# A Mamba block between two ternary feed-forwards: where POOL's u times B stands in each slot

## The reference

```python
x = x + 0.5 * ffn(layernorm(x), W_up, W_gate, W_down)
x = x + mamba(layernorm(x), ...)
x = x + 0.5 * ffn(layernorm(x), W_up, W_gate, W_down)

def ffn(x):            # weights quantised to {-1, 0, 1} * mean(|W|), 2048 hidden units
    hidden = silu(x @ wu.T) * (x @ wg.T)
    return hidden @ wd.T

def mamba(resid):      # E = 1024 channels, N = 16 states per channel
    r = rmsnorm(resid) * norm_w
    skip, x_in = r @ W_skip, r @ W_in
    x = silu(causal_conv4(x_in) + conv_b)
    delta = softplus(x @ W_delta_1 @ W_delta_2 + b_delta_2)
    Bm, Cm = x @ W_B, x @ W_C
    h[l] = h[l-1] * exp(delta[l] * A) + (delta[l] * x[l]) * Bm[l]   # for each e, n
    y[l] = sum_n h[l, e, n] * Cm[l, n]
    return resid + ((y + x * W_D) * silu(skip)) @ W_out
```

## Time and profile before

| | |
|---|---|
| median of 3 runs | 3043.34 us (3043.31 to 3052.29) |
| the profiled execution's own time | 3045.95 us |
| its span, first to last instruction | 3044.2 us |
| busy: PE, DVE, POOL, ACT | 92%, 89%, 65%, 59% |
| chain that ended last: PE, DVE, issue, ACT, POOL | 64%, 20%, 6%, 3%, 1% |
| mean granted TensorE clock | 0.975 |

### The profile page before, as it was taken

The page is one execution under the profiler, slowest core; times in us unless marked ns, Lnnn a source line. Parts: engine busy times, 40 slices in busy tenths (PEclk is TensorE's granted clock), DMA queues, the critical chain, the costliest instruction groups (busy, mean ns, idle before and its releaser), DMA issues.

```text
span 3044.2 us, 53491 instructions
## 1 busy us (share of the span) xinstructions
PE 2796.4 (92%) x18791; PEld 2192.2 (72%) x18791; DVE 2709.3 (89%) x3613; ACT 1809.8 (59%) x4212; POOL 1993.6 (65%) x1875
## 2 busy tenths in 40 slices
PE   4777899999999999999999999999999999999888
PEld 3556677776877777787777768777777877777655
DVE  6359898999999999998999899999999989999992
ACT  6255656565565656556565655656565565656551
POOL 2165676757677675767777576776757677775761
PEclk9888899999999999999999999999999999999888
DMA  6010101001010100101010010101001010100100
GB/s 252 28 32 18 32 22 36 18 22 43 15 39 22 36 18 22 43 17 37 21 36 18 22 43 15 39 22 36 18 22 43 17 38 22 36 18 22 35 29 8
DMA packets 53313, 99.88 MB, mean 33 GB/s; under 512 B 7804, under 2 KB 9144, under 8 KB 52536
## 3 DMA queue, kind: packets, MB, share of 16 engines
q1 hardware_dynamic: 53048, 96.45, 10.1%
HBM read 87.78 MB, written 8.65 MB: 32 GB/s over the span
## 4 chain that ended last, share of the span: by engine, by line
PE 64%; DVE 20%; issue 6%; ACT 3%; POOL 1%; DVEq 0%; ACTq 0%; POOLq 0%
PE ps L1415 17%; PE ps L1426 14%; PE ps L1438 11%; PE ps L1377 10%; DVE h L1164 8%; PE ps L1491 6%; DVE y L1190 4%; DVE xc L1233 2%; PE ps L1447 2%; PE ps L1454 2%; PE ps L1464 2%; DVE act L1206 1%; DVE act L1198 1%; DVE xw L1256 1%; ACT ps L880 1%
## 5 line engine op out<-in xcount | busy, mean ns | idle before, releaser
L647 POOL TENSOR_TENSOR h<-u,bb 128x1024 f32<-128x1024 f32 x512 | 1222.1, 2387 | 305.5 <-PE ps L1377 298.4
L880 ACT ACTIVATE ps<-delta,a_neg 128x255 f32<-128x255 f32 x2048 | 882.4, 466 | 664.1 <-DVE h L1164 662.2
L1164 DVE TENSOR_TENSOR_SCAN h<-ps,h 128x512 f32<-128x512 f32 x1024 | 1191.8, 1205 | 33.3 <-POOL h L651 17.6
L1190 DVE SCALAR_TENSOR_TENSOR y<-ps,ccur,y 128x512 f32<-128x512 f32 x960 | 670.3, 739 | 46.9 <-PE ps L1377 45.9
L1377 PE MATMUL ps<-ident,h 128*128 128x128 f32 x4096 | 564.1, 280 | 97.4 <-DVE y L1190 93.2
L1377 PEld LDWEIGHTS ps<-ident,h 128*128 128x128 f32 x4096 | 475.7, 144 | 183.8 <-issue 80.4
L1415 PE MATMUL ps<-xh,q_gate 128*128 128x256 f16 x2048 | 462.4, 273 | 37.5 <-DVE act L1198 22.6
L1415 PE MATMUL ps<-xh,q_up 128*128 128x256 f16 x2048 | 466.6, 275 | 15.9 <-DVE xl L1103 12.9
L1415 PE MATMUL ps<-xl,q_up 128*128 128x256 f16 x2048 | 466.7, 275 | 0.0
L1415 PE MATMUL ps<-xl,q_gate 128*128 128x256 f16 x2048 | 462.1, 273 | 0.0
L742 POOL TENSOR_TENSOR hl<-act,hh 128x512 f16<-128x512 f32 x256 | 300.9, 1178 | 233.5 <-ACT hh L905 233.5
(11 more groups left out here) (133 smaller groups left out, 3449.4 us busy)
## 6 DMA issues: line engine op xcount, KB each, us to landing
bb<-b_scratch SPq DMA_DIRECT2D x224, 256.0 KB, 3.2
xs<-in_L_attn_resid_dram SPq DMA_DIRECT2D x17, 512.0 KB, 3.8
out_dram<-xs SPq DMA_DIRECT2D x16, 512.0 KB, 4.3
wraw<-in_L_ffn_W_up_dram SPq DMA_DIRECT2D x4, 1024.0 KB, 8.9
wraw<-in_L_ffn_W_gate_dram SPq DMA_DIRECT2D x4, 1024.0 KB, 13.1
wraw<-in_L_ffn_W_down_dram SPq DMA_DIRECT2D x4, 1024.0 KB, 14.2
w_in<-in_L_attn_W_in_dram SPq DMA_DIRECT2D x1, 2048.0 KB, 21.6
w_skip<-in_L_attn_W_skip_dram SPq DMA_DIRECT2D x1, 2048.0 KB, 8.8
```

The lines of the kernel that those rows point to most:

```text
L647: pl.tensor_tensor(h[:, s % RING, :, :], u[:, :, :], bb[:, planes_of(s) % 2, s % PLANES:s % PLANES + 1, :].broadcast_to([P, HE, CH]), ALU. ...
L880: ins = ac.activation(abar[r][:, e, 1:], delta[:, k, 1:], ACT.Exp, scale=a_neg[:, k, n:n + 1])
L1164: v.tensor_tensor_scan(hr, abar[r].rearrange("p e t -> p (e t)"), hr, 0.0, ALU.mult, ALU.add).then_inc(scanned, 1)
L1190: ins = v.scalar_tensor_tensor(out=yy, in0=hT[:, t, :], scalar=cc, in1=yy, op0=ALU.mult, op1=ALU.add)
```

## The change

In each slot of POOL's code, `u_times_b` was first. It now stands behind `edges`, `add_edges`, `rstd` of the second feed-forward, and `hidden_low`; it stays ahead of `rms`, `x12`, `softplus`, `first_state`, `x_times_d` and `rstd` of the next chunk. No instruction is added or removed, no wait is changed, and PE, DVE, ACT and SP keep their order.

```diff
                 for s in range(STEPS):
-                    step = step_of(ph, i, s + U_AHEAD)
-                    if step:
-                        u_times_b(*step)
                     if s == MASK_H and "IN_0" in has:
                         edges(i + 1)
                     for half in range(2):
                         ...
                         rstd(ph, i, "2")
                     for kind, p in hidden_units(ph, s):
                         hidden_low(ph, i, kind, p)
+                    step = step_of(ph, i, s + U_AHEAD)
+                    if step:
+                        u_times_b(*step)
                     if after(ph, "DN1_1", 0, s):
                         rms(ph, i)
```

## The result

| | before | changed |
|---|---|---|
| median, beside each other | 3044.32 us (3043.31 to 3052.29, 4 runs) | 3101.23 us (3099.82 to 3106.23, 4 runs) |
| profiled execution, its span | 3045.95, 3044.2 | 3106.23, 3104.4 |
| busy: PE, DVE, POOL, ACT | 92%, 89%, 65%, 59% | 91%, 88%, 65%, 58% |

The changed kernel is slower by a ratio of 1.0184 [1.0163, 1.0205], 57 us by the medians. 43 us were forecast, and 3101 lies in the range of 3060 to 3106.

The account below looks back on a forecast made before the run. PE and DVE, both nearly full and waiting on each other, were taken as the bound. 14 x (2.2 + 0.6 + 0.1) + 1.3 + 1.0 = 43 us, giving 3086 us against the median of 3043.34; range 3060 to 3106.

Parts of the forecast that it names:

- Place A: Slots 7 to 12 of a loop pass: state 9's product comes late, PE loses 2.2 us a pass, between 0.9 and 3.4.
- Place B: Slots 26 to 28: state 25's product waits behind a late hl, PE loses 0.6 us a pass, between 0 and 2.6.
- slot 20 as covered: Slot 20: u times B waits for the convolution first, but its scan lies over 3 us later; costed at nothing.
- the 0.1 of slots 29 to 31: Slot 30's product may start 0 to 0.2 us late, with softplus behind it: 0.1 us a pass.
- First and last chunk: Last chunk, slot 17: product late for its scan, 1.3 us; first chunk, slot 4, with softplus: 1.0 us, estimated from it.
- The half clock: Rival: PE's new gap in place B drops TensorE's clock each pass, 3105 us; 0.11 together with another slot giving way.
- Hidden: Rival: the product is two slots ahead, so its lateness never reaches PE, 3043 us; chance 0.05.
- faster: Rival: earlier hl and rstd shorten the path POOL, ACT, PE in slots 9 and 10, 3026 us; chance 0.05.
- partly: Rival: only one place costs, or PE's later gaps take some back; half the sum, 3065 us; chance 0.13.

Follow-up runs that it names:

- Slot 10 put back: Changed kernel, with u times B first again in slot 10 of the 14 loop passes: 3079.41 us, ratio 1.0106 to the kernel before.
- the mask's move: Changed kernel, with first_state of the second half in POOL's slot 9 instead of 6: 3092.82 us, ratio 1.0156 to the kernel before.
- slots 25 and 26 put back: Changed kernel, with u times B first again in slots 25 and 26 of the 14 loop passes: 3091.61 us, ratio 1.0149 to the kernel before.
- slot 20 put back: Changed kernel, with u times B first again in slot 20 of the 14 loop passes: 3087.63 us, ratio 1.0131 to the kernel before.
- edges first: Kernel before, with u times B behind the edges only in slot 0 of the 14 loop passes: 3049.32 us, ratio 1.0010.
- slot 10 moved alone: Kernel before, with u times B behind hl only in slot 10 of the 14 loop passes: 3096.94 us, ratio 1.0163.

## Why the prediction was right, and where it was not

The direction, the mechanism and the range were right. A pass at full clock was forecast at +2.9 and measured at +2.96, but that close agreement is partly luck: two missed terms of opposite sign stand in it.

- *Place A, forecast 2.2, measured 1.9 to 2.0.* Each step came nearly as worked out. The wait before state 6's scan is 2.31 (2.3). hh ended 0.3 sooner than put, so state 9's product did too (1490.76, on the old clock 1462.38, against 1462.65). Its scan is 2.0 late, of which the row shows 1.40 as a wait, since DVE itself was 0.5 late; I had given 2.2 for the wait. PE's wait is 1.22 instead of 1.5 to 2, since 0.4 came one slot earlier. Slot 10 put back shows 1.5 of the 2.0, and the mask's move the other half us. Over the run the scans wait 83.5 us for POOL in 59 cases, where some 100 in over 40 were put.
- *Place B, forecast 0.6, measured 0.85* by slots 25 and 26 put back. In chunk 3, at full clock, the steps are there: the scan waits 2.49 (put at 2.5), PE waits 0.47 for the up multiplication before U2_7 (put at 0.5) and is 0.6 later from there on, and of DVE's 2.62 us of idle time 0.95 are left. Another 0.2 comes in the next matmuls, L1464, for a reason that no row names. In chunk 7, where the clock is low, the scan waits 2.05 only.
- *Missed: DVE and POOL block one another.* +1.0 in slot 21 (slot 20 put back shows it) and -0.86 in slot 0 (edges first shows it). I had counted slot 20 as covered because its scan lies 3 us later. That was true of the scan, and beside the point: what a moved instruction runs beside also has a price. The row of 1.16 us for 128x24 integers was in the trace of before, and I did not ask what made it so long. 2.0 + 0.85 + 1.0 - 0.86 = 3.0; the 0.1 of slots 29 to 31 is not to be seen apart.
- *First and last chunk, forecast 2.3 together.* Measured 5.3 and 5.1 for chunks 0 and 15, 8.1 of which the old order there gives back. This is the term of the sum that was most mis-sized: I had looked at one slot in each. In these chunks PE is idle more often (busy 132.26 of 166.5 us in chunk 0 of the changed kernel); that late products in other slots were just as uncovered is likely, but not shown. Which slots, and how much of it is the clock, no run here tells.
- *The half clock*, a rival put at 1.3 us a pass and 19 in all, came in 10 of 13 full passes, mostly at 0.85, 6.6 us net. So a part of that rival's price came, but not for its reason, PE's new gap in place B: in chunk 7 the clock falls at 1578.5, before the hl of place B starts at 1579.05, and with slots 25 and 26 put back 7 of 13 passes still hold it. The forecast's reading that the clock drops where PE has been less busy also rested on too little: in the earlier trace rows PE is busy 7.00 of 7 us in the stretch at 0.81.
- *Hidden, faster, partly* fell. The path POOL, ACT, PE did get shorter (ACT's 1.24 us are gone), but state 9's scan decided.

57 us against 43: in the profiled executions, 13 x 2.96 + 3.9 for the pass of chunk 14 = 42.4 where 40.6 were put; the ends, with what lies before and behind them, 11.3 instead of 2.3, of which nearly 2 are differences between executions that the order has no part in; the half clock 6.6 instead of 0: 60.3 in all, and the changed kernel's profiled execution was its longest, 5 above the median.

## What to carry to other kernels

In an in-order queue the order is a question of which wait stands in front of what: put the instruction whose input is long there ahead of the one that waits, and count the wait, not the work, as the price of the other order. Before moving an instruction of POOL, look also at what DVE runs beside its old and its new place, and at any tiny DVE instruction with a long time. And where a late step has no gap behind it, as here from slot 12 on, a delay of 2.8 us arrives in full (slot 10 moved alone), while removing a wait in front of a busy PE (1.45 us at state 6) brings nothing.

## What was not expected of the hardware

*A DVE instruction that reads two tensors from SBUF and a POOL instruction beside it hold one another up.* L1219 takes 0.16 us alone and 1.16 beside a product, L1242 1.23 and 2.21, L1259 0.69 and 2.15, and POOL's 128x4 addition 0.21 and 1.07. The scans and y_add, of whose two tensor inputs one is in PSUM, kept their 1.2 and 0.7 us beside the same products: over all their executions in the changed kernel they took at most 1.23 and 0.77. The Trainium skill, "SBUF — State Buffer", Terms, calls this a shared port pair, "Lock-allocated, exclusive, held for the full instruction"; its section "SBUF: two separate sides" names DVE's instructions with two SBUF inputs among those that compete for it. The traces agree: the time is not stretched in proportion, it is that to the other's end, with L1242 and L1259 doing about their own work after it. L1219 of chunk 7 before ends at 1399.40 + 1.16 = 1400.56, POOL's product beside it at 1398.17 + 2.35 = 1400.52.

*TensorE at half clock with hardly an idle moment before.* Some falls follow a gap of PE, as that at 520.4 us in the changed kernel and those in slot 12 with slot 10 moved alone. Those in slot 26 don't. Ahead of the stretch at 0.76, PE was busy 20.07 of 21 us, and in the trace of before, where the same slots stayed at 1.00, 20.45 of 21. Its idle time in the 21 us of the changed kernel is a single stretch of 0.93, and in the last 7 us before the fall at 1578.5 it has none. The rows, changed and then before:

```profile
1556.00:1577.00 21.00, 20.07 (x150) 16.74 (x148) 20.58 (x29) 12.67 (x29) 12.22 (x10) 1.00 0.07 23
...
1571.50:1578.50 7.00, 7.00 (x60) 6.59 (x59) 6.65 (x8) 4.19 (x13) 3.69 (x3) 1.00 0.04 13
```
```profile
1526.00:1547.00 21.00, 20.45 (x151) 17.05 (x149) 20.40 (x28) 11.54 (x29) 11.62 (x10) 1.00 0.07 21
```

The kernel with the edges first, whose passes are shorter than those of before, has the half clock more often than it (7 of 13 against 1 or 2). So the length of a pass alone doesn't order the kernels, and what sets off the fall stays open. What the traces do show is its price: 8 of the 11 us that the edges first in slot 0 win in the full passes go to it.
